# Causal attention by pairs of heads in two row halves of TensorE, with its division moved to the mixing stage

## The chip, the core and the metric

The kernel is one program on one core of a Trainium2 chip. The metric is the device time of one execution in microseconds. TensorE is called PE below, VectorE DVE, ScalarE ACT, GpSimd POOL and SyncE SP, as in the rows of the profile. Lines such as L806 are lines of the kernel before, unless the text says otherwise.

## The reference, cut to what the change touches

Two layers over x of shape (2, 2048, 256). The first adds to x a causal attention with 16 query heads of 16 channels (four key and value heads, each shared by four query heads), and a mixture of eight experts. The second adds a sparsemax attention over 32 patterns and a second mixture. The part in question:

```
q = rope((x @ Wqa @ Wqb).reshape(b, s, 16, 16))
k, v = (x @ Wkva @ Wkvb) as 4 heads of 16;  k = rope(k);  each repeated 4 times
scores = einsum('bqhd,bkhd->bhqk', q, k) * 16 ** -0.5
scores = where(causal, -inf, scores)
w = softmax(scores)
out = einsum('bhqk,bkhd->bqhd', w, v).reshape(b, s, 256)
return out @ Wout + bout
```

With two batches that is 32 heads of 2048 queries by 2048 keys, half of them hidden by the causal mask.

## The kernel before

The program runs stage after stage, with all engines waiting for each other between stages: latents (L100 on, 20 to 165 us), routing, `attention` (L586, 199 to 1299 us), the loading of weights for the second layer, the experts, `mixing` (L1489, about 1710 to 1836 us), and the second layer.

**Latents.** In eight chunks of 512 tokens PE makes q and k turned by rope. POOL adds the cosine and sine products (L234), and q and k are cut into three bfloat16 parts, whose sum is the fp32 value: ACT casts the high part (L270), POOL subtracts it, ACT casts the middle part (L274), DVE subtracts that and writes the low part (L401). The parts go to memory as `q_parts` and `k_parts`.

**Attention.** The loop runs over 32 heads. A head has 40 A pieces and 40 B pieces. An A piece (L806) is queries by keys, 128 by up to 512, and serves only to find the row maximum: DVE reduces it (L912). A B piece (L830) is keys by queries, 128 by up to 512, with the negative maximum added by three more rows of the product; ACT takes its exponential into `at_wt` (L778). Scores close to fp32 precision come from six pairs of bf16 parts stacked in 96 rows (99 for B). On the diagonal a second product with the identity adds the causal mask (L809 to A, L833 to B). In one round PE goes through p = 0 to 39 and issues A piece p of the next head and B piece p of this one. Every fourth p it multiplies four finished weight tiles with the values (L850), one key tile into each of four groups of 32 columns of the array, three pieces behind. Both A and B have three PSUM buffers. A group of 512 queries ends in a copy (ACT L770), four transposes (PE L859), a sum over the four column groups, a reciprocal and a multiplication (DVE L947, L950, L955) that writes `s_attn`.

The maximum of each half of the queries is reduced and cut into three parts by five small DVE steps (L929 to L937), turned by PE (L816), copied by DVE (L919) and stored by SP into the rows of `at_qb` (L715). SP loads the operands of the next heads: per head three transfers each for `at_qa` and `at_ka` (L699) and for `at_qb` and `at_kb` (L705), of 48, 32 and 16 rows, and the values (L707, L709). POOL sets the rows of ones and then scatters the 32 token tiles into the experts' buffer (L749, L753), all at the start of the stage.

**Mixing.** A step takes two tiles of 128 tokens. SP loads x and copies the attention rows (`mx_at`, L1579), POOL copies slots and gates (L1589, L1591) and fetches four sets of expert rows by indirect transfers (L1594), PE turns the attention rows (L1610) and multiplies them by the output matrix, and DVE sums and normalises. There are 16 steps.

Of the kernel before, what the change touches and what calls it, by code (L numbers as in the profile page):

```python
# [19 lines left out]
F32 = mybir.dt.float32  # L20
# [26 lines left out]
PARTS = 3  # L47
VW = 32

RUNS = ((0, 3), (3, 2), (5, 1))  # L50
STACK = 6 * D
# [22 lines left out]
def latents(nc, d, s):  # L74

    with ExitStack() as ctx:
# [33 lines left out]
        rest = [sb(f"rest{k}", [P, CH]) for k in range(3)]  # L110
        parts = [sb(f"parts{k}", [P, PARTS, CH], BF16) for k in range(3)]
# [35 lines left out]
        rest_ready = sem("rest_ready")  # L147
        mid_ready = sem("mid_ready")
# [25 lines left out]
        def _(sp):  # L174
# [25 lines left out]
            def chunk(c, u, behind):  # L200
# [5 lines left out]
                for k in range(PAIRS):  # L206
                    sp.wait_ge(low_ready, PAIRS * c + k + 1)
                    dst = d["q_parts"][:, k * P:(k + 1) * P] if k < 2 else d["k_parts"]
                    sp.dma_start(dst[:, :, bass.ds(c * CH, CH)].rearrange("a p n -> p a n"),
                                 parts[k][0:rows_of(k)]).then_inc(parts_out[k], 16)  # L210
# [11 lines left out]
        def _(pool):  # L222
# [7 lines left out]
            def turned(c, k):  # L230

                pool.wait_ge(pair_used, 2 * (PAIRS * c + k) + 6)
# [3 lines left out]
            def left(c, k):  # L236
                pool.wait_ge(high_ready, PAIRS * c + k + 1)
                rows = rows_of(k)
                pool.tensor_tensor(rest[k][0:rows], rot[k][0:rows], parts[k][0:rows, 0],
                                   ALU.subtract).then_inc(rest_ready, 1)  # L240
# [7 lines left out]

            rounds(pool, chunk)
# [3 lines left out]
        def _(act):  # L253
# [13 lines left out]
            def high(c, k):  # L267
                act.wait_ge(rot_ready, PAIRS * c + k + 1)
                act.wait_ge(parts_out[k], 16 * (c + 1))
                act.copy(parts[k][0:rows_of(k), 0], rot[k][0:rows_of(k)]).then_inc(high_ready, 1)  # L270

            def mid(c, k):
                act.wait_ge(rest_ready, PAIRS * c + k + 1)
                act.copy(parts[k][0:rows_of(k), 1], rest[k][0:rows_of(k)]).then_inc(mid_ready, 1)  # L274

            def chunk(c, u, behind):
# [4 lines left out]
                mid(c, 0)  # L281
# [3 lines left out]
                mid(c, 1)  # L285
                if behind >= 2:
                    std_of(c + 2)
                mid(c, PAIRS - 1)
# [79 lines left out]
        def _(dve):  # L368
# [22 lines left out]
            def products(c, u, k):  # L391
# [3 lines left out]
                dve.wait_ge(pair_made, n + 1)  # L395
                dve.tensor_tensor(by_cos[k][0:rows], pR[m][0:rows, 0], cos[0:rows, at], ALU.mult).then_inc(pair_used, 1)
                dve.tensor_tensor(by_sin[k][0:rows], pR[m][0:rows, 1], sin[0:rows, at], ALU.mult).then_inc(pair_used, 1)

            def low(c, k):
                dve.wait_ge(mid_ready, PAIRS * c + k + 1)  # L400
                dve.tensor_tensor(parts[k][0:rows_of(k), 2], rest[k][0:rows_of(k)], parts[k][0:rows_of(k), 1],  # L401
                                  ALU.subtract).then_inc(low_ready, 1)

            def chunk(c, u, behind):
# [6 lines left out]
                low(c, 0)  # L411
                if ahead:
                    variances(c + 2)
                low(c, 1)
                if ahead:
                    normalise(c + 2, u, c // 2 + 2)
                low(c, 2)
# [2102 lines left out]
```

## Time and profile before

| | us |
|---|---|
| three runs | 2589.8, 2591.25, 2599.59 |
| median | 2591.25 |
| profiled execution, span from first to last instruction | 2609.7 |
| attention in it | 199.4 to 1299.0 |
| PE busy over the whole span | 2234.0 (86%) |
| DVE, ACT, POOL busy | 1772.8, 1179.7, 772.4 |

The profiled execution has no other time than its span. It is 0.7% above the median. In a row of the timeline the first number is the start in us from the start of the span, the second the time until the end of the last of the instructions that the row groups, and xN their number. A product of the values has two records (L850: 2496 for 1248 products). A PE record is longer than the distance from one product to the next, since products are pipelined, so the rate of PE is read from the distance of starts. PEld is the loading of weights for the product that follows.

### The profile page before, as it was taken

What the parts mean: (1) busy time and instruction counts of PE and PEld (TensorE: products, weight loads), DVE (VectorE), ACT (ScalarE), POOL (GpSimd) and SP (SyncE); (2) the same over time, 40 slices, a digit from 0 to 9 for tenths busy, and PEclk for the clock granted to TensorE, in tenths of its full rate; (3) what the DMA queues carried; (4) which work ended last, traced back from release to release, by engine and by line L of the source; (5) the groups of instructions that cost most, each with busy time, mean ns of one, the idle gap of its engine ahead of it and who ended that gap; (6) DMA issues with size and microseconds to landing.
All of it is one profiled execution on the core that took longest, in us unless ns stands there. A gap on an engine that the chain in (4) does not pass through costs nothing. (4 is left out here: it accounts for less than half of the span.)

```text
span 2609.7 us, 44812 instructions
## 1 busy us (share of the span) xinstructions
PE 2234.0 (86%) x12898; PEld 1283.6 (49%) x12898; DVE 1772.8 (68%) x3458; ACT 1179.7 (45%) x2552; POOL 772.4 (30%) x613
## 2 busy tenths in 40 slices
PE   5866889999999999999879999967578887798777
PEld 2322333333333333333369999946345544454446
DVE  3656667778887778777433333346498889988892
ACT  1222556666666666666644454411123333343332
POOL 3333333000000000000023333355156666566651
PEclk9756989999999999999989999976689898898897
DMA  7423333111111111111142223156400000000004
GB/s 280 130 70 104 96 104 103 57 56 58 58 58 56 58 56 58 57 57 57 30 146 94 97 81 109 49 159 196 145 1 16 17 17 0 16 16 16 9 0 141
DMA packets 140179, 191.32 MB, mean 73 GB/s; under 512 B 19256, under 2 KB 116416, under 8 KB 137920
## 3 DMA queue, kind: packets, MB, share of 16 engines
q1 hardware_dynamic: 111392, 139.92, 16.6%
q0 software_dynamic: 9120, 31.47, 3.7%
q10 hardware_dynamic: 19584, 18.88, 2.1%
q8 instruction: 46, 0.75, 0.1%
q14 instruction: 37, 0.30, 0.0%
HBM read 125.34 MB, written 60.29 MB: 71 GB/s over the span
## 5 line engine op out<-in xcount | busy, mean ns | idle before, releaser
L912 DVE TENSOR_REDUCE at_piece_max<-at_A 128x1 f32<-128x512 f32 (+3 forms) x1280 | 740.9, 605 | 249.3 <-PE at_A L809 205.9
L778 ACT ACTIVATE at_wt<-at_B 128x512 f32<-128x512 f32 (+3 forms) x1280 | 607.9, 537 | 339.1 <-PE at_B L833 211.9
L806 PE MATMUL at_A<-at_ka,at_qa 96*128 96x512 bf16 (+3 forms) x1280 | 459.1, 361 | 79.2 <-DMA at_ka<-k_parts 76.2
L830 PE MATMUL at_B<-at_qb,at_kb 99*128 99x512 bf16 (+3 forms) x1280 | 446.2, 353 | 1.7 <-ACT at_wt L778 0.6
L850 PE MATMUL at_O<-at_wt,at_v 128*32 128x512 f32 (+3 forms) x2496 | 339.2, 548 | 0.4 <-ACT at_wt L778 0.4
L806 PEld LDWEIGHTS at_A<-at_ka,at_qa 96*128 96x128 bf16 x1280 | 126.2, 99 | 432.7 <-DVE at_piece_max L912 245.8
L1176 POOL TENSOR_TENSOR s_down<-lw_down_full,s_down 128x256 fp32r<-128x256 f32 x10 | 7.3, 729 | 873.9 <-ACT lw_down_full L1168 873.9
L1353 PE MATMUL ex_H<-ex_xT,ex_w_in 128*128 128x256 f32 x1920 | 247.5, 285 | 3.2 <-DVE ex_xT L1460 3.2
L1353 PEld LDWEIGHTS ex_H<-ex_xT,ex_w_in 128*128 128x128 f32 x1920 | 236.6, 192 | 3.6 <-DVE ex_w_out L1465 3.6
L2051 POOL TENSOR_TENSOR l_sumy<-l_sumy,l_scaled 128x1024 f32<-128x1024 f32 x72 | 220.1, 3057 | 27.9 <-ACT l_scaled L2201 26.6
L2251 DVE TENSOR_TENSOR l_order<-l_order 128x1024 f32<-128x1024 f32 x112 | 221.2, 1975 | 1.9
L1474 DVE TENSOR_TENSOR ex_h<-ex_act_a,ex_H 128x256 f32<-128x256 f32 x160 | 67.0, 419 | 226.6 <-ACT ex_act_a L1402 226.5
L2252 DVE TENSOR_TENSOR l_order<-l_order 128x1024 f32<-128x1024 f32 x112 | 211.0, 1884 | 0.0
L2041 POOL TENSOR_TENSOR l_hT<-l_h,l_hT 128x512 fp32r<-128x512 f32 x80 | 135.4, 1692 | 235.4 <-ACT l_hT L2180 235.4
L2180 ACT CAST l_hT<-l_h 128x512 fp32r<-128x512 f32 x80 | 49.5, 618 | 329.3 <-DVE l_h L2275 329.3
L1395 POOL TENSOR_TENSOR ex_hT<-ex_h,ex_hT 128x256 fp32r<-128x256 f32 x160 | 119.4, 750 | 256.1 <-ACT ex_hT L1406 256.1
L2133 PE MATMUL l_D<-s_down,l_hT 128*128 128x256 f32 x960 | 161.5, 326 | 37.5 <-POOL l_hT L2041 35.4
L2133 PEld LDWEIGHTS l_D<-s_down,l_hT 128*128 128x128 f32 x960 | 140.0, 218 | 71.1 <-POOL l_hT L2041 41.4
L830 PEld LDWEIGHTS at_B<-at_qb,at_kb 99*128 99x128 bf16 x1280 | 126.1, 99 | 87.6 <-ACT at_wt L778 11.9
L2111 PE MATMUL l_G<-s_attn,s_gate_up 128*128 128x512 f32 (+1 forms) x320 | 157.5, 616 | 0.0
L2116 PE MATMUL l_U<-s_attn,s_gate_up 128*128 128x512 f32 (+1 forms) x320 | 150.4, 592 | 0.0
L2080 PE MATMUL l_Z<-s_to_scores,l_xT_score 128*128 128x512 f32 x128 | 77.9, 740 | 72.3 <-DVE l_z L2233 68.6
(246 smaller groups left out, 3191.2 us busy)
## 6 DMA issues: line engine op xcount, KB each, us to landing
buf<-zeros POOLq DMA_DIRECT2D x10, 1024.0 KB, 20.6
ex_x<-buf SPq DMA_DIRECT2D x40, 256.0 KB, 2.7
expert_out<-ex_y ACTq DMA_DIRECT2D x40, 256.0 KB, 2.2
at_v<-v SPq DMA_DIRECT2D x32, 256.0 KB
ex_raw_in<-in_W_in SPq DMA_DIRECT2D x8, 1024.0 KB, 4.9
q_parts<-parts SPq DMA_DIRECT2D x16, 384.0 KB, 4.5
at_qa<-q_parts SPq DMA_DIRECT2D x32, 192.0 KB
at_ka<-k_parts SPq DMA_DIRECT2D x32, 192.0 KB
```

The lines of the kernel that those rows point to most:

```text
L778: act.activation(wt[p % NE_][:, q0:CH], pB_of(p, u)[:, q0:CH], ACT.Exp, scale=D ** -0.5).then_inc(wt_ready, 1)
L806: ins = pe.matmul(pA[b][:, 0:w], qa[u][:, i * P:(i + 1) * P], ka[u][:, k0:k0 + w], start=True, stop=not diag)
L830: ins = pe.matmul(pB_of(p, u)[:, q0:CH], kb[u][:, kt * P:(kt + 1) * P], qb[u][:, j * CH + q0:(j + 1) * CH], start=True, stop=not diag)
L850: ins = pe.matmul(pO[j % 2][VW * g:VW * (g + 1), q0:CH], vs[u][:, kt // TPC, kt % TPC, :], wt[p % NE_][:, q0:CH], start=kt < 4 and j > 0, ...
L912: dve.tensor_reduce(piece_max[:, i, k0 // CH:k0 // CH + 1], pA[a_step(p) % NA][:, 0:w], AX.X, ALU.max).then_inc(a_used, 1)
L1353: ins = pe.matmul(pH[f][:, a, :], w_in[w][wq][:, k, cols], xT[i][xq][:, k, :], start=(n == 0), stop=(n == len(terms) - 1))
L2051: pool.tensor_tensor(sumy[u][:], sumy[u][:], buffer(u, i)[:], ALU.add).then_inc(sum_step, 1)
L2111: ins = pe.matmul(pG[i % 2][:], s["gate_up"][:, e, k, :], xT[:, k, bass.ds(c * CH, CH)], start=(k == 0), stop=(k == EC - 1))
L2116: ins = pe.matmul(pU[i % 2][:], s["gate_up"][:, e, EC + k, :], xT[:, k, bass.ds(c * CH, CH)], start=(k == 0), stop=(k == EC - 1))
L2133: ins = pe.matmul(pD[q][:, t, :], hT[m % 2][hq][:, cols], s[f"down{wq}"][:, ORDER[m], :], start=(n2 == 0), stop=(n2 == len(terms) - 1))
L2251: dve.tensor_tensor(dv[:, :, 0:half], low, high_m, ALU.max).then_inc(sort_step, 1)
L2252: dve.tensor_tensor(dv[:, :, half:size], high, low_m, ALU.min).then_inc(sort_step, 1)
```

## The change

Attention now runs over 16 pairs of heads in place of 32 heads. One head of a pair sits in partitions 0 to 63 of the operands and one in 64 to 127, so that the two products of a pair use two row halves of PE's array. The parts are two fp32r values instead of three bf16 ones, and the stack has three terms of 16 rows: 48 rows for A and 50 for B. There are 40 steps p in a pair as there were in a head, each with two A and two B products. The products with the identity are gone. The mask of A is added on DVE, in the reduction itself (32 of the 80 pieces of a pair, two instructions each); the mask of B is laid over the exponentials by POOL (32 selects of 128x128 in a pair). A group of values is now two key tiles of two heads, every second p. Four fp32 products with a 0/1 matrix turn and sum at once, and ACT copies numerators and sums of weights into `s_attn`. The maximum is cut in three steps instead of five. `q_parts` and `k_parts` hold two f32 values where there were three bf16 ones. There are 16 buffers for `at_wt` instead of 8, with the same three for A and three for B. SP issues 12 transfers for the A operands of a pair and 13 for B and the values, each of 16 rows by 2048 f32. The rows of ones are loaded by four SP transfers, queued behind the loads of the first pair and the A loads of the second, and PE waits for them ahead of its first product. POOL fetches and scatters two token tiles in each pair. In the latents stage ACT's middle cast and DVE's subtraction are gone, and POOL writes the low part. In mixing DVE takes one reciprocal of all sums, and POOL multiplies, in place of SP's copy of `mx_at`.

PE in a round, before. `at_hide` with `at_identb` is the mask product:

```order
L850 MATMUL at_O<-at_wt,at_v 32x512 x4
L806 MATMUL at_A<-at_ka,at_qa 128x512
L809 MATMUL at_A<-at_hide,at_identb 128x128
L830 MATMUL at_B<-at_qb,at_kb 128x128
L833 MATMUL at_B<-at_hide,at_identb 128x128
L806 MATMUL at_A<-at_ka,at_qa 128x512
L830 MATMUL at_B<-at_qb,at_kb 128x512
L806 MATMUL at_A<-at_ka,at_qa 128x512
L830 MATMUL at_B<-at_qb,at_kb 128x512
```

The same place in the program changed, in its own line numbers (826 is A, 847 is B, 865 the values):

```order
L865 MATMUL at_O<-at_wt,at_v 32x512 x4
L826 MATMUL at_A<-at_ka,at_qa 128x512 x2
L847 MATMUL at_B<-at_qb,at_kb 128x128 x2
L826 MATMUL at_A<-at_ka,at_qa 128x512 x2
L847 MATMUL at_B<-at_qb,at_kb 128x512 x2
L865 MATMUL at_O<-at_wt,at_v 32x512 x2
L865 MATMUL at_O<-at_wt,at_v 32x384 x2
```

Products of A and of B come in twos, and a group of values stands after two steps instead of four.

SP at the start of the changed attention stage, from the last loads for the second pair on:

```order
L683 DMA at_qa<-q_parts 16x2048
L683 DMA at_ka<-k_parts 16x2048
L715 DMA at_kb<-at_ones 2x4x512 x4
L698 DMA at_qb<-at_max_rows 2x8x128 x4
L688 DMA at_qb<-q_parts 16x2048
L688 DMA at_kb<-k_parts 16x2048
```

The four transfers of ones stand behind 37 loads (12, 13 and 12).

POOL in two steps of mixing, before:

```order
L1589 COPY mx_at_slot<-s_slot_get 128x4
L1591 COPY mx_gate<-s_gates 128x4
L1594 DMA mx_ye<-expert_out,mx_at_slot 128x256 x4
L1589 COPY mx_at_slot<-s_slot_get 128x4
L1591 COPY mx_gate<-s_gates 128x4
```

and changed:

```order
L1578 COPY mx_at_slot<-s_slot_get 128x4
L1580 COPY mx_gate<-s_gates 128x4
L1583 DMA mx_ye<-expert_out,mx_at_slot 128x256 x4
L1589 TENSOR_TENSOR mx_at<-s_attn,mx_over_sum 128x512
L1578 COPY mx_at_slot<-s_slot_get 128x4
L1580 COPY mx_gate<-s_gates 128x4
```

The multiplication that makes `mx_at` stands behind the four indirect fetches of its step.

The diff, cut to its core:

```diff
-PARTS = 3
+PARTS = 2
-RUNS = ((0, 3), (3, 2), (5, 1))
-STACK = 6 * D
+Q_TERMS, K_TERMS = (0, 0, 1), (0, 1, 0)
+STACK = len(Q_TERMS) * D
+HP = 2
+BASE = P // HP
+HPAIRS = B * H // HP
...
-            def mid(c, k):
-                act.wait_ge(rest_ready, PAIRS * c + k + 1)
-                act.copy(parts[k][0:rows_of(k), 1], rest[k][0:rows_of(k)]).then_inc(mid_ready, 1)
...
-            def low(c, k):
-                dve.wait_ge(mid_ready, PAIRS * c + k + 1)
-                dve.tensor_tensor(parts[k][0:rows_of(k), 2], rest[k][0:rows_of(k)], parts[k][0:rows_of(k), 1],
-                                  ALU.subtract).then_inc(low_ready, 1)
...
-        NA, NB, NE_ = 3, 3, 8
+        NA, NB, NE_ = 3, 3, 16
...
             load_a(0, 0)
             load_b(0, 0)
             load_a(1, 1)
-            max_store(0, 0, 0, M0_AT + 3)
+            sp.wait_ge(ones_made, 1)
+            for u in range(2):
+                for h in range(HP):
+                    rows = kb[u][BASE * h + STACK:BASE * h + QKS, :]
+                    sp.dma_start(rows.rearrange("a (j n) -> a j n", n=CH).bitcast(F32),
+                                 ones[:].bitcast(F32).unsqueeze(1).to_broadcast([MR, NQ, CH])).then_inc(ones_in, 16)
...
+            def causal(n, p, h):
+
+                j, kt, q0 = Bp[p]
+                N = PER_B * n + HP * p + h
+                block_ = wt[(HP * p + h) % NE_][:, q0:q0 + P]
+                pool.wait_ge(wt_ready, N + 1)
+                pool.affine_select(block_, block_, [[1, P]], ALU.is_ge, 0.0, base=0,
+                                   channel_multiplier=-1).then_inc(hidden, 1)
...
+            def keep(n, j):
+                G = NQ * n + j
+                act.wait_ge(oT_made, G + 1)
...
+                act.copy(dst, src).then_inc(o_kept, 1)
...
+            pe.wait_ge(ones_in, 16 * 4)
...
+                wait(pe, a_used, PER_A * n + a_slot(p, HP - 1) - NA + 1)
+                for h in range(HP):
+                    rows = slice(BASE * h, BASE * h + STACK)
+                    pe.matmul(pA[a_slot(p, h) % NA][:, 0:w], qa[u][rows, i * P:(i + 1) * P], ka[u][rows, k0:k0 + w],
+                              start=True, stop=True).then_inc(a_made, 1)
...
+                    ins = pe.matmul(pX_of(j)[:, t, :], raw[j % 2][:, t * P:(t + 1) * P], summing[:], start=True, stop=True)
...
+                if diagonal:
+                    ins = dve.tensor_tensor_reduce(junk[(HP * i + h) % 4][:, 0:w], pA[slot % NA][:, 0:w], hide[:, CH - w:CH], 1.0, NEG,
+                                                   ALU.add, ALU.max, accum_out=top)
+                else:
+                    ins = dve.tensor_reduce(top, pA[slot % NA][:, 0:w], AX.X, ALU.max)
...
-                sp.dma_start(at[u][:], s["attn"][:, bass.ds(2 * t, 2), :]).then_inc(x_in[u], 16)
...
+                wait(pool, aT_made, t - 1)
+                both = bass.ds(2 * t, 2)
+                pool.tensor_tensor(at[u][:].rearrange("p w (h n) -> p w h n", n=D), s["attn"][:, both, :, 0:D],
+                                   over_sum[:, both].unsqueeze(3).to_broadcast([P, 2, H, D]),
+                                   ALU.mult).then_inc(at_ready, 1)
```

## Rows read from the trace of the kernel before

**Rows 1.** Page, part 2: granted PE clock and memory traffic in 40 slices
```profile
PEclk9756989999999999999989999976689898898897
...
GB/s 280 130 70 104 96 104 103 57 56 58 58 58 56 58 56 58 57 57 57 30 146 94 97 81 109 49 159 196 145 1 16 17 17 0 16 16 16 9 0 141
```

**Rows 2.** Busy times in stretches: attention, latents, mixing, start of attention
```profile
core 0: us, PE busy (x) PEld busy (x) DVE busy (x) ACT busy (x) POOL busy (x), PEclk, DMA share, GB/s
...
212.00:216.00 4.00, 1.45 (x9) 0.94 (x9) 0.96 (x3) 0.00 (x0) 0.31 (x1) 0.50 0.57 179
476.00:1260.00 784.00, 755.27 (x5128) 305.72 (x5127) 622.64 (x1549) 504.37 (x1065) 0.00 (x0) 0.99 0.18 58
20.00:162.00 142.00, 125.64 (x271) 51.91 (x272) 73.86 (x174) 38.14 (x79) 53.24 (x43) 0.79 0.47 163
...
```

**Rows 3.** Groups by line, 476 to 1260 us: A products that start there
```profile
L806 PE MATMUL at_A<-at_ka,at_qa 96*128 96x512 bf16 (+2 forms) x968 | 341.0, 352 | 27.7 <-DMA at_ka<-k_parts 25.6 <-DVE at_piece_max L912 2.0
```

**Rows 4.** Timeline inside one round of attention, around 700 us
```profile
701.86 0.60 PE L859 MATMUL at_O<-s_ident,at_raw 128*128 128x128 f32 x4
...
703.08 1.07 PE L850 MATMUL at_O<-at_wt,at_v 128*32 128x512 f32 x8
...
704.08 0.39 PE L806 MATMUL at_A<-at_ka,at_qa 96*128 96x512 bf16 x1
...
704.51 0.69 DVE L912 TENSOR_REDUCE at_piece_max<-at_A 128x1 f32<-128x512 f32 x1 [0.64 <-PE at_A L806]
...
707.43 5.06 DVE L912 TENSOR_REDUCE at_piece_max<-at_A 128x1 f32<-128x512 f32 x8 [0.37 <-PE at_A L809]
...
707.57 0.38 PE L830 MATMUL at_B<-at_qb,at_kb 99*128 99x512 bf16 x1
...
707.79 0.38 PE L806 MATMUL at_A<-at_ka,at_qa 96*128 96x512 bf16 x1
...
707.98 1.57 ACT L778 ACTIVATE at_wt<-at_B 128x512 f32<-128x512 f32 x3 [0.16 <-PE at_B L830]
```

**Rows 5.** Groups with shapes kept apart, 600 to 800 us: maximum and PE
```profile
L912 DVE TENSOR_REDUCE at_piece_max<-at_A 128x1 f32<-128x512 f32 x175 | 115.3, 685 | 18.8 <-PE at_A L809 12.2 <-PE at_A L806 3.8
...
L806 PEld LDWEIGHTS at_A<-at_ka,at_qa 96*128 96x128 bf16 x248 | 24.1, 97 | 72.8 <-DVE at_piece_max L912 50.7 <-issue 6.2 <-DVE at_max_rows L919 5.0
...
L809 PE MATMUL at_A<-at_hide,at_identb 128*128 128x128 bf16 x99 | 21.8, 220 | 0.0
...
L912 DVE TENSOR_REDUCE at_piece_max<-at_A 128x1 f32<-128x128 f32 x25 | 7.2, 286 | 5.9 <-PE at_A L809 5.1
```

**Rows 6.** Timeline in the experts: fp32r products with 128 rows
```profile
1499.74 3.52 PE L1353 MATMUL ex_H<-ex_xT,ex_w_in 128*128 128x256 f32 x28
```

**Rows 7.** Timeline at the two ends of attention
```profile
200.26 2.12 SPq L699 DMA_DIRECT2D at_qa<-q_parts  x3
...
214.55 0.26 PE L806 MATMUL at_A<-at_ka,at_qa 96*128 96x128 bf16 x1 [23.00 <-DMA at_ka<-k_parts]
...
239.74 0.29 PE L806 MATMUL at_A<-at_ka,at_qa 96*128 96x128 bf16 x1 [3.66 <-DMA at_ka<-k_parts]
...
1298.75 0.22 DVE L955 TENSOR_TENSOR s_attn<-at_osum,at_oinv 128x64 f32<-128x64 f32 x1
```

**Rows 8.** Groups by line, whole span: kinds of DVE and POOL work
```profile
L234 POOL TENSOR_TENSOR rot<-by_cos,by_sin 128x512 f32<-128x512 f32 (+1 forms) x24 | 30.9, 1292 | 84.3 <-DVE by_sin L397 84.3
...
L1696 DVE TENSOR_TENSOR mx_part<-mx_W,mx_part 128x512 f32<-128x512 f32 x16 | 10.9, 680 | 7.5 <-PE mx_W L1616 7.4
...
L931 DVE CAST at_max_parts<-at_neg_max 128x8 bf16<-128x8 f32 x64 | 10.3, 161 | 0.0
```

**Rows 9.** Timeline in mixing: POOL's last fetch of a step, PE, POOL's next copy
```profile
1782.98 1.18 POOL L1594 DMA_INDIRECT mx_ye<-expert_out,mx_at_slot  x1 [0.30 <-issue]
...
1783.62 0.64 PE L1610 MATMUL mx_A<-s_ident,mx_at 128*128 128x128 f32 x4
...
1784.43 0.18 POOL L1589 COPY mx_at_slot<-s_slot_get 128x4 uint32 x1 [0.27 <-issue]
```

More of the change, by code:

```diff
@@ L109, in latents @@
         rot = [sb(f"rot{k}", [P, CH]) for k in range(3)]
-        rest = [sb(f"rest{k}", [P, CH]) for k in range(3)]
-        parts = [sb(f"parts{k}", [P, PARTS, CH], BF16) for k in range(3)]
+        parts = [sb(f"parts{k}", [P, PARTS, CH], F32R) for k in range(3)]
         vtok = [sb(f"vtok{u}", [P, KVH, TPC, VW]) for u in range(2)]
@@ L876, in round_ @@
                         elif not first:
[L877 removed]
+                            values(n - 1, 1 - u, NPC + p - 1 - LAG)
                     for j in range(NQ):
[L879 to L883 removed]
+                        late = j == NQ - 1
@@ L924, in cut_max @@
-                base = 5 * (2 * n + half)
+                t = slice(half * HALF_T, (half + 1) * HALF_T)
+                base = 3 * (2 * n + half)
                 if step:
@@ L959, in _, with round_ @@
-            CUT_1 = {0: (0,), 1: (1, 2), 2: (3, 4)}
-            CUT_0 = {HALF[0] + k: (k,) for k in range(5)}
-            def round_(n, first, ahead):
+            CUT_1 = {0: 0, 1: 1, 2: 2}
+            CUT_0 = {HALF + k: k for k in range(3)}
+            def round_(n, ahead):
                 for p in range(NPC):
                     if ahead:
-                        maximum(n + 1, p)
-                    for step in CUT_1.get(p, ()):
-                        cut_max(n, 1, step)
+                        for h in range(HP):
+                            maximum(n + 1, p, h)
+                    if p in CUT_1:
+                        cut_max(n, 1, CUT_1[p])
@@ L977, in round_ @@
-                    for j in range(NQ):
-                        step = (p - END[j] - LAG - 3) % NPC
-                        if step < 3:
-                            if j < NQ - 1:
-                                result(n, j, step)
-                            elif not first:
-                                result(n - 1, j, step)
+                    if ahead and p in CUT_0:
+                        cut_max(n + 1, 0, CUT_0[p])
+                    if ahead and p == M0_AT:
+                        max_copy(n + 1, 0, PER_A * (n + 1) + M0_SLOT, M0_SLOT % NA)
@@ L1005, in layer1_weights @@
+            for n in range(HPAIRS):
+                round_(n, n + 1 < HPAIRS)
 def layer1_weights(nc, d, s):
```

453 lines of the change are left out of this document (215 added, 238 removed).

## The prediction

> **What bounds the kernel now.** I read the busy times in stretches first, since only attention's inner loop changes. From 476 to 1260 us PE is busy 755.27 of 784.00 us at a granted clock of 0.99, that is at the 2.4 GHz level, DVE 622.64 and ACT 504.37 [rows 2]. 968 of the 1280 A pieces start there [rows 3], 24.2 heads of 40 pieces, so a round takes 784.00/24.2 = 32.4 us a head, 64.8 for two heads. PE is full by its records, but they overlap. What it does is read from the distances of starts: an A and a B product of 512 columns stand 0.22 us apart (707.57 to 707.79), a group of values takes 1.00 to 1.07 (703.08 to 704.08), and the four transposes 0.60 for the four [rows 4]. The idle time of PE's weight loads ahead of A products is 72.8 us in 200, 50.7 of it for DVE's reduction to release a buffer [rows 5]. DVE reduces 512 columns in 685 ns, and in a run of eight one every (5.06−0.68)/7 = 0.62, ACT's exponential every (1.57−0.60)/2 = 0.49 [rows 4, 5]. So PE's order bounds the round, and the coupling A product, reduction, next A product through three buffers costs a part of it.
>
> **Time of a changed round.** Call T the time of one pair (two heads, 64.8 now).
>
> Removed from PE, per pair: 2 × 32 mask products (2 × 16 of A, 2 × 16 of B). Behind a piece of fewer than 512 columns they cost little more than their start; their records are 220 ns long but overlap [rows 5].
>
> PE's two row halves: a pair of A products reads 48 rows at 0 and 48 at 64. fp32r products of 256 columns with 128 rows follow each other, loads included, every (3.52−0.28)/27 = 0.12 us [rows 6]. So 512 columns are 0.24, and if the halves work side by side the pair costs 0.24 for two products, plus a few hundredths. The trace has the same kind of thing in columns: eight records of the values, four column groups, 1.07 us [rows 4]. I take side by side. Serial would be 0.48 a pair, and never more than the 0.53 of one pass of 512 columns in the values (eight records in 1.07 over four groups); both are rivals below.
>
> The buffers: three A buffers now serve two pieces per step. The next pair needs the first piece of the pair before released: 0.43 from the product's start to the reduction's (704.08 to 704.51), 0.68 for the reduction, 0.05 to wake PE: 1.16 us for 512 columns. A reduction gets about 0.13 shorter with every 128 columns (685 ns for 512, 286 for 128 [rows 5]), so with 384, 256 and 128 it is 1.03, 0.90 and 0.77; over the 40 steps (24 off the diagonal and 16 on it, four of each width) the mean is (24×1.16 + 4×(1.16+1.03+0.90+0.77))/40 = 1.08. Within that time lies the B pair of the first step.
>
> Per two steps: 1.08 from the first A pair to the second, 0.48 for the second A and B pair, and a group of values. It now comes every second step with the same four products; 1.07 each for 16 of 20, and 0.63 (column counts of diagonals are shorter) for 4: mean 0.98. Sum 2.54, times 20 = 50.8. Sixteen summing products at 0.15 (0.60/4) and their wakening, 3.5; two turns of the maximum and waits around them, 0.6. **T = 55.**
>
> DVE's own load in a pair is 48 plain reductions, 0.60 apart at best, and 32 masked ones. A masked one is unknown: it reads PSUM and SBUF and has a second instruction. An addition of 512 columns from PSUM takes 680 ns [rows 8], like the reduction of 685, and a small DVE instruction 161 [rows 8]. From below it costs nothing more than the plain one, from above 0.16 more. With 0.10 more, over its mean of shorter widths, 0.50: 28.8 + 16.0 + 1.5 for cuts and copies = 46.3. ACT: 80 exponentials as before and four copies, 36. Both under 55, so they stay covered while PE takes 55; if PE were free DVE would come next at 46 to 49.
>
> POOL's mask of B is a new link: exponential, select, values. POOL took 1.29 us for 512 columns of two inputs [rows 8] and 0.18 for a copy of 4 columns [rows 9]: for 128 columns 0.46 by a straight line between them; bounds 0.2 and 0.75 for one select. Two are needed per diagonal step of 2.5/2 = 1.27 us, so it decides only above about 0.6 and hurts only when the three steps of lag (about 3.8 us) are used up, which at 0.85 begins. Four indirect scatters of about 1 us stand in POOL's queue at step 12 of each pair, ahead of the selects from step 20 on: eight steps, 10 us, cover their 5. I take nothing.
>
> SP issues 25 loads in a pair; three loads take 2.12 us to issue [rows 7], 0.71 each, 18 us of 55. The two stores of the maximum stand behind them, as one stood before; no wait is added beyond that.
>
> **The start and the end.** First product 214.55, first transfer about 200 [rows 7]. Now PE waits for the ones, behind 37 loads of 131 KB: 4.85 MB. The traffic of the start is 179 GB/s in 212 to 216 us [rows 2]; the page's highest slice is 280, the slices of the first rounds 96 to 104 [rows 1]. By issue alone 37 × 0.71 = 26 us. At 150 GB/s, chosen since the stretch of 179 holds POOL's traffic too, 32, and 4 for the ones and the memory round trip: first product at 199.4 + 36.6 = 236. Bounds 26 and 50. The Trainium skill, "DMA: Bandwidth & Descriptors", section "Why a DMA increments its semaphore by 16 and not by 1", says that a transfer uses as many engines, up to 16, as divide its slowest dimension. By that rule the loads before, whose slowest dimension is 3 or 2 parts, use three or two engines, and those of 16 rows all 16; the start would then be near its lower bound, ten us less. No row here tells engines apart.
>
> The first A round without B ran from 214.55 to about 236 (next head's loads in at 239.74 [rows 7]), at a clock of 0.50 [rows 2]; for two heads and DVE's 0.62 a piece 46 us. Then 15 rounds of 55 = 825, a last round without A 37, the tail 4. Attention: 36.6 + 46 + 825 + 37 + 4 = 949, now 1298.97−199.4 = 1099.6: **−150.**
>
> **Latents.** PE is busy 125.64 of 142 us at 0.79 [rows 2], so what ACT and DVE lose was beside it; −2 (bounds −10 from the shorter chain, +3 from the new waits and from values of 4/3 the bytes to store).
>
> **Mixing.** The multiplication stands behind four fetches. The last ended at 1782.98 + 1.18 = 1784.16, and PE's turn (L1610) of this period began at 1783.62 [rows 9]. POOL's 512 columns take 1.29 [rows 8], so PE can start at 1785.9 with waking, 2.3 later, and POOL's next copy, at 1784.43 [rows 9], goes 1.3 later. If all of POOL's delay carries, +1.25 a step; 16 steps: **+20.** Bounds +8 (a part hidden by the step ahead) and +35 (2.3 each). The reciprocal of 32×16 sums once, +1, is in it.
>
> Sum: −150 −2 +20 = −132 of the profiled 2609.7, so 2478. On the median of the runs shown, 2591.25 − 132 = **2460.** The case's own range: T from 52 to 58, start and mixing bounds, 2410 to 2510.
>
> **The rivals.**
> (B) *Row halves one after the other.* A and B pairs cost 0.44 to 0.48 in place of 0.24: 0.4 more per two steps, 8 a pair, T = 63. For it: no row shows two row halves. Against: the column groups overlap. 2460 + 15×8 + 5 = 2585.
> The Trainium skill, "TensorEngine Tiling (Array Packing)", Key Properties, says that tiles work in parallel on both loads and products, and that a change of tiling drains the array. By the first T is 55, by the second each of 40 changes a pair between rows and columns costs a drain; the trace has such changes between 96 rows and column groups already, inside the 0.98 to 1.07.
> (C) *The coupling is hidden.* If reductions release sooner than I think (the values fall into the wait), only DVE's 46 to 49 remains. For it: 0.48 of B lies in the 1.08. T = 49: 15×6 = 90 less, about 2365.
> (D) *Slower than before: four-byte pairs stream as the values do.* Place: the products of L826 and L847. Price: a pass of 512 columns of the values takes 0.53; with that per pair, 0.29 more each for the second A and B pair and 0.29 on the gap, 0.87 per two steps, 17.4 a pair: T = 72, 15×17.4 = 261: about 2720. Against it stands 0.12 for 256 columns [rows 6]. It decides from T = 55 + 132/15 = 63.8 on.
> (E) *POOL's select is slow*, 1.2 us as if 512 columns: 32 × 1.2 per pair come in bursts of eight, 9.6 us of select for 5 of steps, four times, half of it not absorbed by the lag: +9.5, T = 64.5, about 2600.
>
> **How the numbers follow.** Forecast 0.50; B 0.13; C 0.12; D 0.12; E 0.08; others (code loading of the unrolled DVE and POOL loops, clock) 0.05. About 0.5% (13 us) is what a measurement can tell from no change: 2578 to 2604. Faster: forecast, C and a part of B and E, 0.72. Same: the rest of B and E, 0.10. Slower: D and others, 0.18. The range leaves out D and a little on the low side: 2385 to 2620.
>
> **What would show it.** A pair's distance of A products in the timeline: 1.1 and 1.46 in turn. If A and B products of a pair start within 0.05, the halves overlap; 0.22 speaks for B, 0.5 for D. Idle time of PE before A named to DVE's reduction confirms the coupling; named to POOL, E. The masked reduction at 0.6 to 0.8 us; the select at 0.46. First A product at 236, mixing steps of 8.8 in place of 7.5. I would be wrong if the granted clock in the rounds, 0.99 now, fell to the 1.2 GHz level because PE now waits at every step, though each wait would be under 0.7 us; the first round already runs at 0.50 after its idle start.

## The result

The changed kernel takes 2804.32 us (median of four, 2771.72 to 2828.78) against 2594.73 for the kernel before in four runs. The ratio is 1.0707, with a 95% interval of 1.0644 to 1.0770: 7% slower, where 5% faster was forecast. That ratio, like all ratios with an interval below, leaves out slow runs, those over 1.5% above the kernel's fastest, here the two above 2793.19 us; the medians of all four give 1.081. The profiled execution is the longest of the four and has a span of 2827.0 us, 217.3 more than the 2609.7 of before. The mean granted clock of the four runs was 0.781 to 0.801, lower in the longer ones; that spread is part of what is explained below.

Page of the changed kernel, part 2, which answers to [rows 1]:

```profile
PEclk9555559568765698878557999995778889999897
```

Slices 4 to 21 of 40 are attention. Before they read 9 nearly throughout; now they go up and down between 5 and 8, with 9 in two of them.

Busy times in stretches of the changed kernel, for [rows 2] (PE, PEld, DVE, ACT, POOL with the number of instructions, then the granted clock, the DMA share and GB/s):

```profile
309.00:1431.00 1122.00, 981.67 (x5356) 387.00 (x5348) 684.68 (x1766) 612.68 (x1322) 214.31 (x572) 0.72 0.38 55
417.00:476.00 59.00, 49.23 (x361) 20.22 (x360) 46.16 (x121) 40.62 (x88) 14.24 (x38) 1.00 0.31 45
476.00:561.00 85.00, 77.31 (x361) 30.41 (x360) 46.91 (x121) 40.91 (x88) 14.27 (x38) 0.58 0.49 73
```

The first row is attention's rounds together: clock 0.72, where it was 0.99 from 476 us on [rows 2] and 0.98 over all rounds. The second and third are one round each, with the same 361 PE records. The first of them ran at the 2.4 GHz level and took 59 us, the next mostly at 1.2 GHz and took 85. DVE and ACT are busy for nearly the same time in both. Their bounds are products that turn a half's maximum, the first of the two in each pair:

```profile
416.78 0.28 PE L833 MATMUL at_A<-s_ident,at_max_parts 128*32 128x128 f32 x1
...
475.73 0.28 PE L833 MATMUL at_A<-s_ident,at_max_parts 128*32 128x128 f32 x1
...
560.47 0.39 PE L833 MATMUL at_A<-s_ident,at_max_parts 128*32 128x128 f32 x1
```

The 15 rounds took 58.8 to 95.9 us, 73.7 on average, against 55 forecast. Two heads took 64.8 before from 476 us on, and 66.4 over all rounds.

Where the 217 us come from, by stage. Attention starts at 184.5 and not 199.4 (−15) and lasts 1308.2 in place of 1099.6 (+209). From its end to the last turn in mixing it is 556.4 in place of 532.7 (+24). The rest is unchanged.

Timeline of the changed kernel at full clock, for [rows 4]:

```profile
705.92 0.50 PE L826 MATMUL at_A<-at_ka,at_qa 48*128 48x512 f32 x2
...
706.46 1.29 DVE L935 TENSOR_REDUCE at_piece_max<-at_A 128x1 f32<-128x512 f32 x2 [0.59 <-PE at_A L826]
...
707.21 0.44 PE L826 MATMUL at_A<-at_ka,at_qa 48*128 48x384 f32 x2 [0.54 <-DVE at_piece_max L935]
...
707.48 0.39 PE L847 MATMUL at_B<-at_qb,at_kb 50*128 50x512 f32 x2
...
707.79 0.56 DVE L932 CUSTOM_DVE_ANT_0 at_junk<-at_A,at_hide 128x384 bf16<-128x384 f32 x1
...
707.80 1.07 PE L865 MATMUL at_O<-at_wt,at_v 128*32 128x512 f32 x8
...
708.58 0.29 POOL L755 TENSOR_SCALAR_AFFINE_SELECT at_wt<-at_wt 128x128 f32<-128x128 f32 x1 [7.89 <-ACT at_wt L794]
...
708.80 0.50 PE L826 MATMUL at_A<-at_ka,at_qa 48*128 48x512 f32 x2
```

Two products of a pair end together in 0.44 to 0.50 us: the row halves do work side by side. The A pair at 707.21 reaches DVE at 707.79, 0.58 later. PE stood idle 0.54 us ahead of it, waiting for DVE's reduction. This happens at nearly every second step: in the round from 417 to 476 us PE waits 17 times for the maximum's work, 9.6 us in all, 0.84 at the longest.

### The profile page after: what moved, and what is told of

Its sections match the earlier page's. It is cut to its first block and busy times, and to the rows that moved or that the text cites. A ratio compares the mean times of both kernels' runs of the same rounds, so it can differ in the third digit from the quotient of the medians.

```text
span 2827.0 us, 40157 instructions
## 1 busy us (share of the span) xinstructions
PE 2290.6 (81%) x11842; PEld 1297.9 (46%) x11842; DVE 1691.8 (60%) x3306; ACT 1150.4 (41%) x2526; POOL 930.2 (33%) x1140
## 5 line engine op out<-in xcount | busy, mean ns | idle before, releaser
L794 ACT ACTIVATE at_wt<-at_B 128x512 f32<-128x512 f32 (+3 forms) x1280 | 615.1, 532 | 662.9 <-PE at_B L847 649.2
L935 DVE TENSOR_REDUCE at_piece_max<-at_A 128x1 f32<-128x512 f32 x768 | 494.1, 686 | 253.7 <-PE at_A L826 252.6
L826 PE MATMUL at_A<-at_ka,at_qa 48*128 48x512 f32 (+3 forms) x1280 | 376.9, 586 | 217.8 <-DVE at_piece_max L932 80.8
L755 POOL TENSOR_SCALAR_AFFINE_SELECT at_wt<-at_wt 128x128 f32<-128x128 f32 x512 | 146.0, 293 | 1054.6 <-ACT at_wt L794 1047.4
L826 PEld LDWEIGHTS at_A<-at_ka,at_qa 48*128 48x128 f32 x1280 | 149.6, 231 | 662.6 <-DVE at_piece_max L935 348.6
L865 PE MATMUL at_O<-at_wt,at_v 128*32 128x512 f32 (+3 forms) x2560 | 431.9, 727 | 0.0
L932 DVE CUSTOM_DVE_ANT_0 at_junk<-at_A,at_hide 128x128 bf16<-128x128 f32 (+3 forms) x512 | 230.6, 488 | 230.4 <-PE at_A L826 228.6
L847 PE MATMUL at_B<-at_qb,at_kb 50*128 50x512 f32 (+3 forms) x1280 | 315.9, 491 | 13.5 <-ACT at_wt L794 13.0
L847 PEld LDWEIGHTS at_B<-at_qb,at_kb 50*128 50x128 f32 x1280 | 159.4, 246 | 71.5 <-ACT at_wt L794 56.0
```

The source lines that it names most:

```text
L794: act.activation(wt[(HP * p + h) % NE_][:, q0:CH], pB_of(p, h, u)[:, q0:CH], ACT.Exp, scale=D ** -0.5).then_inc(wt_ready, 1)
L826: pe.matmul(pA[a_slot(p, h) % NA][:, 0:w], qa[u][rows, i * P:(i + 1) * P], ka[u][rows, k0:k0 + w], start=True, stop=True).then_inc(a_made, 1)
L847: pe.matmul(pB_of(p, h, u)[:, q0:CH], kb[u][rows, kt * P:(kt + 1) * P], qb[u][rows, j * CH + q0:(j + 1) * CH], start=True, stop=True).then ...
L865: pe.matmul(pO[j % 2][rows, q0:CH], vs[u][:, kt // TPC, kt % TPC, :], wt[(HP * p + h) % NE_][:, q0:CH], start=kt < 2 and not late, stop=kt ...
L932: ins = dve.tensor_tensor_reduce(junk[(HP * i + h) % 4][:, 0:w], pA[slot % NA][:, 0:w], hide[:, CH - w:CH], 1.0, NEG, ALU.add, ALU.max, ac ...
L935: ins = dve.tensor_reduce(top, pA[slot % NA][:, 0:w], AX.X, ALU.max)
```

## The experiments

Ratios are each to the kernel before on the same chip. The diffs show one place where there are several alike. The theories: **K**, PE's waits at each step lower its clock; **U**, a sharper K, what counts is how much of PE's array is at work, in rows as well as in time; against them **W**, the instructions themselves are slower; and later **J**, only one long stall per two pairs does it.

**1. Useless work in the waits, in two sizes.**

```diff
+            def filler(j):
+                for g in range(4):
+                    pe.matmul(pO[j % 2][VW * g:VW * (g + 1), 0:FILL], blank[:], hide[:, 0:FILL], start=False, stop=False)
```

> The changed kernel with useless work added: in 16 of the 20 steps of a pair that have no group of values, PE also issues four products of 512 columns with weights of zeros, one per group of 32 columns, into the sums that are open (they add zero). Theory K (clock): the changed rounds are slow because PE, waiting for DVE at each step, is granted 1.2 GHz for much of attention (0.72 on average over 1122 us); filling the waits keeps it at 2.4 GHz. Then a round is the 59 to 62 us of the undisturbed rounds plus what the filler adds beyond the wait (about 0.4 us at 16 places, 6 us): about 67 in place of 76, attention's clock above 0.9, the kernel about 2660. Rival W (work): the rounds are long because the instructions themselves take longer (four-byte products, masked reductions, selects); then 16 x 1.07 us more of PE work add 0.4 to 1.0 us at each place, 6 to 17 us a pair, and the kernel is 2900 to 3050. Rival H (heat or power of four-byte products): the clock falls further, over 2900.

> The same filler with 256 columns, about 0.53 us at each of the 16 places, which is about the wait there. Theory K: the clock rises as with 512 columns or a little less, and the filler costs nothing beyond the wait: rounds of 60 to 63 us, the kernel 2570 to 2620. Rival W: no gain, 2790 to 2850. Rival H: slower.

Measured: 2787.54 us with 512 columns (ratio 1.0704, 1.0647 to 1.0761), 2736.97 with 256 (1.0509, 1.0464 to 1.0554). The clock over 309 to 1240 us is 0.90 with 256 columns and 0.93 with 512, against 0.72 without. W and the rival of power fall: more work raised the clock, and with 256 columns shortened the kernel. But both sizes missed the times that K gave. Rounds were 67 to 78 us with 512 and 65 to 83 with 256, and even the rounds of 65.3, at a clock of 0.97, are longer than the 59.0 at 1.00 without filler. So K was right in direction, and this filler was too dear to show what the clock alone is worth. Part of it isn't the filler's length: in each of those rounds PE has one wait of 2.4 to 2.5 us for DVE, which the changed kernel's rounds don't have; its cause was not looked for.

**2. The two heads in one row half, one after the other.**

```diff
-                    rows = slice(BASE * h, BASE * h + STACK)
+                    rows = slice(0, STACK)
```

> Both products of a pair read the first head's 48 or 50 rows, so they use the same row half and follow one another (the second head's scores are left out, so its output is not the reference's). PE's work for scores doubles: 0.24 us more for each of 80 pairs of products. Theory K: PE is busier, the clock stays at 2.4 GHz most of the time, and a round is about 60 + 8 to 10 = 70 us, under the 76 of the changed kernel: about 2700. Rival W: 80 x 0.24 = 19 us a pair more at most, 8 at least: 2930 to 3100.

Measured: 3391.66 us (ratio 1.3044, 1.3005 to 1.3083), a first round of 80.3 us and 14 of 111.6 to 114.2. K as I had put it falls, and W's range was passed as well. The busy times in a stretch of this kernel:

```profile
309.00:1240.00 931.00, 920.92 (x2970) 467.65 (x2969) 385.75 (x997) 341.63 (x729) 120.19 (x316) 0.50 0.29 41
```

PE is busy 920.92 of 931.00 us, 99%, more than in the kernel before and in the changed one, and yet its clock is 0.50 throughout. The time that PE is busy doesn't keep the clock up.

**3. The same products with nearly all rows.** The kernel of experiment 2 with 112 rows read in place of 48 and 50. The operand buffers are set to zero before the first load.

```diff
-                    rows = slice(0, STACK)
+                    rows = slice(0, BASE + STACK)
```

> The serial kernel (e3_serial) once more, but each of the two products of a pair reads 112 rows: both heads' 48 and the 16 between them, which are set to zero. The scores of the two heads are added up, so the output is not the reference's. Number, widths and order of products are those of e3_serial, which ran all of attention at 0.50 with PE busy 99% of the time and 111.6 us a round. Theory U (use of the array): the clock follows how much of the array works, rows too, and not how long PE is busy; then these rounds run at 2.4 GHz: 68 to 75 us, the kernel about 2700 to 2750. Rival S (the serial order or four-byte products are what the clock falls for): it stays at 0.50 and about 111 us a round, 3390.

Measured: 2708.78 us (ratio 1.0393, 1.0359 to 1.0428), rounds of 65.4 to 72.4. The same stretch:

```profile
309.00:1240.00 931.00, 873.57 (x4935) 456.19 (x4928) 636.55 (x1645) 561.95 (x1211) 194.90 (x516) 0.99 0.44 65
```

Same order of instructions, same columns, only more rows: clock 0.99 in place of 0.50, 683 us less. This is the run that decides for U. (It doesn't tell whether the number of rows counts or the use of both halves: 112 rows do both.) It also says what the row halves are worth. In this kernel the two products of a pair follow one another with their full cost, and a round takes 66.1 us at a clock of 1.00; with the halves side by side it takes 58.8 and 59.0. An A, a B and an A pair there:

```profile
700.58 0.74 PE L827 MATMUL at_A<-at_ka,at_qa 112*128 112x512 f32 x2
701.16 0.52 PE L848 MATMUL at_B<-at_qb,at_kb 112*128 112x384 f32 x2
701.87 0.72 PE L827 MATMUL at_A<-at_ka,at_qa 112*128 112x512 f32 x2 [0.19 <-DVE at_piece_max L938]
```

**4. Fewer rows in the kernel before.**

```diff
-                ins = pe.matmul(pA[b][:, 0:w], qa[u][:, i * P:(i + 1) * P], ka[u][:, k0:k0 + w],
+                ins = pe.matmul(pA[b][:, 0:w], qa[u][0:48, i * P:(i + 1) * P], ka[u][0:48, k0:k0 + w],
```

> The kernel before with one thing changed: A products read 48 of their 96 rows, B products 35 of 99 (the rows of the maximum among them); parts of the scores are left out, so the output is not the reference's. Every instruction stays, with its columns. Theory U: rounds fall to the 1.2 GHz level for much of attention although PE is busy as before; at 0.5 a head would take 50 to 55 us in place of 32.4, the kernel 3000 to 3300; if the clock alternates, 2750 to 3000. Rival S: no change, 2595 to 2605, clock 0.90.

Measured: 2690.52 us (ratio 1.0323, 1.0284 to 1.0363). Neither expectation holds: slower than S gave, less so than U. From 260 to 440 us the granted clock is 0.82 (0.91 in the kernel before), and rounds there take up to 49 us; later it is 0.99 and nearly every round takes 34.0 to 34.6 against 31.5 to 34.7. The timeline shows why it was no clean test:

```profile
709.64 0.39 PE L806 MATMUL at_A<-at_ka,at_qa 48*128 48x512 bf16 x1
709.65 0.39 PE L830 MATMUL at_B<-at_qb,at_kb 35*128 35x512 bf16 x1
709.87 0.32 PE L806 MATMUL at_A<-at_ka,at_qa 48*128 48x384 bf16 x1
710.12 0.23 PE L809 MATMUL at_A<-at_hide,at_identb 128*128 128x128 bf16 x1
710.29 0.39 PE L830 MATMUL at_B<-at_qb,at_kb 35*128 35x512 bf16 x1
```

The rows that I had left to B lie in the other half of the array (64 to 98), so an A and a B product start 0.01 us apart and run side by side, and more of the array works than I had meant. And a change between a product of a half and one of all rows seems to cost time: a mask product of 128 columns holds the next back by 0.17 us (710.12 to 710.29), where in the kernel before one B mask and the A product behind it start 0.06 apart:

```profile
707.29 0.22 PE L833 MATMUL at_B<-at_hide,at_identb 128*128 128x128 bf16 x1
707.35 0.38 PE L806 MATMUL at_A<-at_ka,at_qa 96*128 96x512 bf16 x1
```

The changed kernel has such changes at every group of values, but no price shows there: from a group's start to the next A product it is 1.00 us (707.80 to 708.80), as before (703.08 to 704.08 [rows 4]). The Trainium skill, "TensorEngine Tiling (Array Packing)", Key Properties, says both, that tiles work independently and that changing the tiling drains the array; these rows agree with both.

**5. One part of the change alone, in the kernel before:** B's mask by POOL.

```diff
-                if diag:
-                    ins = pe.matmul(pB_of(p, u)[:, q0:q0 + P], identb[:], hide[:, 1], start=False, stop=True)
...
+                        pool.affine_select(block_, block_, [[1, P]], ALU.is_ge, 0.0, base=0,
+                                           channel_multiplier=-1).then_inc(hidden, 1)
```

> One part of the change alone, in the kernel before: the 512 mask products of B are gone and POOL lays the mask over the exponentials, with its token tiles spread over the heads. Theory K and U: a mask product costs PE only its start and 128 columns, 0.055 to 0.1 us at 16 places a head, 0.9 to 1.6 us of 32.4, if the clock stays at 0.99: 30 to 50 us less, about 2560. Rival: a round is held by the coupling with DVE's reductions, whose load is 79%, and nothing is gained: 2590 to 2600. A second rival: POOL's select (0.29 us measured, 4 behind each other at the end of a group) delays the values and with them the A products, 5 to 20 us more.

Measured: 2647.64 us (ratio 1.0165, 1.0141 to 1.0189), slower by 43 where 30 to 50 less was expected. From 309 to 1254 us the clock is 0.94 (0.98 before), and PE waits longer at each head's start for the keys:

```profile
L825 PE MATMUL at_A<-at_ka,at_qa 96*128 96x512 bf16 (+3 forms) x894 | 323.0, 364 | 63.4 <-DMA at_ka<-k_parts 63.4
```

63.4 us for 22 heads, 2.8 each, against 27.7 for 24 [rows 3]. That accounts for 1.7 us a head, more than the whole loss of 43 us over 31 rounds, 1.4 each. The clock falls behind these waits (0.58 from 297 to 301 us, behind the one that ends at 295.9), so its loss comes with them. The run changes two things, since the token tiles are also spread over the heads. The kernel before has a hint of what that does: while its POOL scatters, to 447 us, PE waits 2.3 to 4.9 us for the keys at each head, 27.5 us for seven heads up to 476 us, and 25.6 for all 24 after that. So the scatters' traffic may be what holds the keys back in every head here; the spread alone wasn't run, so this isn't shown.

**6. Order of two queues,** in the changed kernel: ones ahead of the loads, POOL's multiplication ahead of the fetches.

```diff
+            sp.wait_ge(ones_made, 1)
+            for u in range(2):
...
             load_a(0, 0)
             load_b(0, 0)
             load_a(1, 1)
-            sp.wait_ge(ones_made, 1)
...
+                if not isinstance(t, int) or t > 0:
+                    divided(t, u)
                 wait(pool, sums, 6 * (t - 1))
```

> Two changes of order in two stages. SP sends the rows of ones ahead of the 37 loads; and in mixing POOL's multiplication stands ahead of the four fetches of its step (behind them in the first), with DVE's reciprocal ahead of the wait for constants. PE's first product was at 227.6 us in the changed kernel, 43 after the stage began. Expected: first product about 22 us after it (12 loads at 0.46 to issue and 14 to land), 20 us saved; mixing back from 125.2 us between first and last turn to about 113, and its first turn 8 us earlier: 15 to 20 saved. Together 35 to 40 of about 2804. Theory K and rival W agree here; a rival for the start is that the first A round is then held by the loads of its own operands, and gains under 5.

Measured: 2834.0 us (ratio 1.0938, 1.0868 to 1.1008): not faster. Yet the two places gained what was expected. The first product stands 20.0 us after the stage's first transfer instead of 43.1, and from attention's end to the last turn of mixing it is 537 instead of 556. The rounds in between, 63.3 to 92.7 us with the same instructions, took more than that back: 77.1 on average in place of 73.7, at a clock of 0.73 over 309 to 1240 us. The changed kernel's own four runs spread over 57 us. In it the clock's ups and downs are larger than 40 us, and a gain elsewhere can't be read from the total. Why they came out worse in all four runs here is open.

**7. A cheap filler, with the order of experiment 6, and without it.**

```diff
+            def filler(j):
+                for _ in range(FILL):
+                    pe.matmul(pO[j % 2][:], blank_b[:, 0:P], blank_b[:], start=False, stop=False)
```

> The changed kernel with the order of e4_order (ones first, multiplication first) and another filler: at the 16 steps without values PE issues two bf16 products of 128 rows by 128 columns by 512 with zero weights into the open sums, 0.43 us together at full clock, in place of the eight records of 0.53. Theory U: they use the whole array, so the clock rises as with e2_fill256 or more (0.89 over 309 to 1431 there), at less time: rounds of 61 to 65, kernel 2600 to 2680. If zeros or bf16 do not count for the clock, it stays at 0.72 and 2780 to 2830.

> The changed kernel with the bf16 filler alone: loop, order of the ones and order in mixing are its own. Beside e8_best it gives the worth of the two changes of order: first product 18 us earlier and mixing about 15 shorter, so 2588 + 33 = about 2620. Beside the changed kernel (2804) it gives the worth of the clock: 180 to 200 us. If the order is worth nothing, 2590.

Measured: 2588.37 us (ratio 0.9923, 0.9897 to 0.9948; under the 2600 to 2680 expected) and 2641.4 (1.0113, 1.0094 to 1.0132; on another chip, so the ratios are compared). Two bf16 products with zero weights and zero data in 16 waits of a pair bring the ratio from 1.0707 to 1.0113, 154 us on 2595, where 180 to 200 were expected, and the clock over 309 to 1240 us from 0.72 to 0.94. The gain isn't in the rounds' own work: at a clock of 1.00 a round with this filler takes 60.2 or 60.3 us, longer than the 58.8 and 59.0 without. The order is worth 1.9%, 49 us, once the clock is steadier (33 expected). Most rounds of the kernel with both are 60.2 to 61.7, and from the fifth to the thirteenth every second one is 68 to 75. The timeline in the fifth:

```profile
517.89 0.60 PE L873 MATMUL at_O<-at_blank_b 128*128 128x512 bf16 x2
521.05 0.33 PE L828 MATMUL at_A<-at_ka,at_qa 48*128 48x128 f32 x2 [2.56 <-issue]
```

PE does nothing for 2.56 us, and the profile names nothing it waits for. It stands where PE's loop jumps back, and experiment 8 tests that. There are five such stalls, of 2.46 to 2.99 us, one per two pairs. The changed kernel has three, and longer ones:

```profile
599.51 0.47 PE L826 MATMUL at_A<-at_ka,at_qa 48*128 48x128 f32 x2 [4.87 <-issue]
```

The clock in the tens of microseconds around it:

```profile
510.00:520.00 10.00, 8.09 (x54) 2.31 (x52) 7.71 (x17) 5.49 (x13) 2.26 (x8) 1.00 0.01 3
520.00:530.00 10.00, 7.18 (x36) 3.16 (x38) 4.04 (x19) 3.57 (x9) 2.27 (x8) 0.62 0.02 4
530.00:540.00 10.00, 9.79 (x49) 4.62 (x45) 3.83 (x12) 3.58 (x8) 0.00 (x0) 0.50 0.01 2
540.00:550.00 10.00, 10.00 (x42) 4.49 (x42) 3.84 (x10) 4.09 (x10) 1.74 (x6) 0.50 0.93 123
550.00:560.00 10.00, 9.46 (x58) 3.14 (x55) 7.54 (x22) 6.53 (x14) 4.55 (x6) 0.84 1.07 132
560.00:570.00 10.00, 9.81 (x65) 3.71 (x63) 7.33 (x18) 6.23 (x15) 2.00 (x7) 1.00 0.83 143
```

The clock falls with the stall and stays at 1.2 GHz for some 30 us, though PE is busy 98% and 100% of the time by its records. That is the longest of the five: it fell at the other four too, and came back after some 14 us. In the changed kernel it also fell where there is no jump: 1.00 from 480 to 490 us, 0.52 from 490 to 500.

**8. PE's loop written out,** with the filler, without it, and in the kernel before.

```diff
-            with pe.Fori(1, HPAIRS // 2 - 1) as j:
-                for u in range(2):
-                    round_(2 * j + u, u, False, True)
-            round_(HPAIRS - 2, 0, False, True)
+            for n in range(2, HPAIRS - 1):
+                round_(n, n % 2, False, True)
```

> e8_best with PE's loop over pairs written out, so that PE has no jump every second pair. In e8_best PE stands still for 2.6 to 3.0 us at that jump (put down to nothing the profile shows), the granted clock falls to 0.50 for some 30 us after it, and the pair takes 67 to 75 us in place of 61.7. If the jump causes the stall: all rounds 60 to 62 us, attention's clock above 0.97, the kernel 40 to 50 us faster than e8_best, about 2545. Rival: the stall is a wait for something else, or the fetch of written-out code stalls as much: 2580 to 2610.

> e9_unrolled without the filler: e4_order with PE's loop written out. This tells apart what lets the clock fall. Theory U (the waits at every step leave too little of the array at work): the clock in attention stays under 0.85, rounds between 59 and 90 us, the kernel 2700 to 2830. Rival J (only the long stall at the jump does it, and the filler merely hid that): rounds of 59 to 60 us throughout and the kernel about 2520, the best of all.

> The kernel before with PE's loop over heads written out, the fair partner of e9_unrolled. Its rounds alternate between about 31.9 and 32.4 to 34.7 us. If the jump costs it 1 to 2 us at 15 places: 2570 to 2585. If its wait at that place is for the loads of the next head's keys, as the profile names it: no change, 2595 to 2605.

All but the kernel before have the order of experiment 6. Measured: with the filler 2558.55 us (ratio 0.9793, 0.9766 to 0.9820; about 2545 expected), all rounds after the first 60.1 to 61.7, and no stall of that kind left. Without it 2718.89, within what U gave, and its four runs lie between 2677.81 and 2782.58. The kernel before, written out, 2598.76 (0.9949, 0.9929 to 0.9969), 13 us less. That is within its rival's 2595 to 2605, and its waits for the keys are as long as before (43.2 us from 309 to 1254 us, 45.5 before), so in that kernel no cost of the jump is shown. The same stretch with the filler and without:

```profile
309.00:1240.00 931.00, 868.69 (x5915) 338.84 (x5913) 663.75 (x1720) 626.30 (x1352) 215.63 (x576) 0.99 0.43 64
```

```profile
309.00:1240.00 931.00, 803.77 (x4871) 324.20 (x4871) 630.68 (x1634) 554.39 (x1197) 193.24 (x518) 0.82 0.41 61
```

J falls as the whole cause: without the jump, the clock is still 0.82 and rounds go from 58.7 to 91.5. Nor are the waits the whole: with the filler, the jump cost 1.3%, and without it some 5% (medians of all runs 2834.0 and 2718.89, each to its kernel before: 1.089 and 1.041). Both pull the clock down. With both gone the new scheme beats the kernel before by 2.1%, and the written-out kernel before by 1.6% (0.9793/0.9949). But 1.9% of that is what the order of experiment 6 was worth. With the order that was forecast, the scheme at a steady clock would by this come out about even with the kernel before, not 5% under it; that kernel wasn't run.

## Why the prediction was wrong

**The step that failed** is the one at the very end of the prediction: that the granted clock of 0.99 would hold, since each wait is under 0.7 us. The waits are nearly that short (0.54 us at 707.21, 0.84 at the longest), and the clock was 0.72. The clock's fall stood there as a sign of being wrong, and that sign came; but I had priced rounds from distances at 2.4 GHz and left the clock among "others" with a part of a chance of 0.05. The removal of PE's work was counted only as a gain. Before, 64 mask products and 96-row products of 0.22 us filled PE's time to 96%; the change halves the time of the scores and leaves 49 us of busy records in a round of 59. The Trainium skill, "TensorE: Matmul & The Clock Gate", Part 1, says that the gate goes by how busy PE has been; experiment 2 disagrees with this read literally (busy 99%, clock 0.50), and experiment 3 shows that rows count: clock 0.99 with 112 in place of 48 and 50.

Of the 359 us by which attention missed its forecast (1308.2 against 949), the 15 rounds with both A and B are 294 (1119 against 825). At the 58.8 of full clock they would have missed by 57, so some 240 are the clock's. The rest is the start (+6.5), the first A round (227.6 to 288.6, 61.0 against 46) and what follows the last A product (84.7 against 37 + 4). In the written-out kernel with the filler, whose clock is steady from the second round on, that end still took 56.1 us, and the first A round, again at 0.50, took 61.2: those two terms were too small by 15 us each.

**T at full clock** was 55 forecast, and 58.8 and 59.0 measured in the changed kernel's two rounds at a clock of 1.00 (62.0 in three at 0.93 to 0.94). The mechanism stood: the second A pair of two steps waits for the first pair's reduction (0.54 <-DVE), so rival C, a hidden coupling, is out. Two terms were too small. From product to reduction it is 0.53 to 0.58 us and not 0.43, so the distance from the first A pair to the second is 1.29 (705.92 to 707.21) and not 1.16. And a pair of 512 columns takes 0.32 to 0.34 (707.48 to 707.80) and not 0.24, so the distance to the next step's pair is 1.59 (707.21 to 708.80) and not 1.46. Together 0.26 per two steps, which would be 5 us a pair if all steps were so wide; with the summing products below that would make 7, and T missed by 4. The narrower steps were not taken apart. The 0.32 to 0.34 is nearer to side by side (0.24) than to one after the other (0.48 forecast; 0.58 in experiment 3, from 700.58 to 701.16), so rival B is out, and so is D as I put it, by streaming at 0.53. That D's sign came true and its size nearly (2804 against 2720) is luck: it came by the clock, not by D's mechanism. At a clock of 0.50 to 0.51 a round takes 91.4 and 95.9 us.

**The summing products** were priced by the four transposes, 0.15 each. They have two records each, eight in 1.10 us (at 702.82): 4.4 a pair in place of 2.4.

**DVE and POOL** held. A masked reduction of 384 columns takes 0.48 to the next, with 0.08 for its second instruction; one select 0.29 us (0.46 taken, bounds 0.2 and 0.75). The busy time of DVE in a round is 46.2 us (46.3 taken), of ACT 40.6 (36 taken). Rival E is out: values wait for the select 2.8 us in all.

**The start**: forecast 36.6 from the stage's start to the first product, measured 43.1, within the bounds of 26 and 50. The 37 loads were issued in 17.3 us (26 taken), and the wait is for the landing. The profile names the ones:

```profile
227.63 0.47 PE L826 MATMUL at_A<-at_ka,at_qa 48*128 48x128 f32 x2 [50.95 <-DMA at_kb<-at_ones]
```

The Trainium skill, "DMA: Bandwidth & Descriptors", section "Why a DMA increments its semaphore by 16 and not by 1", has the rule on the number of engines from which the prediction worked out ten us less. That gain did not come.

**Mixing**: +20 forecast. The stretch from first to last turn grew from 113.1 to 125.2 us, and the first turn came 8.4 later after the end of the experts, 20.5 together. The second part wasn't in my sum: DVE's reciprocal takes 3.35 us and POOL's first step stands behind it, and the carry-over per step was 0.8 and not 1.25. PE waited for POOL:

```profile
L1589 POOL TENSOR_TENSOR mx_at<-s_attn,mx_over_sum x16: 1061/1063/1073, 1922.7 to 2046.6; 128x512 f32 x14, 128x512 f32<-128x512 f32 x2
...
  PE mx_A L1605: 31.7, 10
```

**Latents**: −2 forecast, −15 measured (bounds −10 and +3). But one execution of each says little here. Attention starts at 178.4 to 191.1 us in ten kernels with the changed latents code, median 185.6, and at 187.0 to 199.4 in four with the code of before (experiments 4, 5 and 8, and the kernel before), median 192.3. The two ranges overlap, and the medians differ by 7 us, within the bounds. So the −15 is in part the kernel before's late start in its profile. Which of the removed steps gave the rest wasn't tried.

## What to carry to other kernels

Work taken from PE can slow it: where PE then waits for another engine at each step, look at the granted clock of the changed kernel first, and price a forecast at both levels before trusting a saving. Products with few rows in one half kept the clock at 0.50 with PE busy 99%, so don't take PE's busy share as a sign that the clock will hold. A wait that can't be removed may be filled with a cheap product of all rows with zero weights into an open sum, sized to the wait and no longer; and a loop's jump on PE costs more than its own 2.5 to 3.0 us if the clock falls with it. When the clock is unsteady, judge another gain by its own stage and not by the total.

## What was not expected of the hardware

- PE busy 99% of 931 us with products of 48 and 50 rows and groups of values between them: granted clock 0.50 throughout. The same with 112 rows: 0.99, and 3391.66 us became 2708.78.
- After a stall of 2.56 us the clock stayed at the 1.2 GHz level for about 30 us, with PE busy 98% to 100%. After four more such stalls in the same kernel it was about 14 us.
- Two bf16 products of 512 columns with zero weights and zero data at 16 waits a pair, some 7 us of work in 60, raised the granted clock from 0.72 to 0.94 and took the ratio to the kernel before from 1.0707 to 1.0113.
- Products of rows 0 to 47 and of rows 64 to 98 run side by side also where they belong to different matrices (starts at 709.64 and 709.65).
